# Side products on TensorE in two halves and farther apart: an attention layer whose softmax exponentials run back to back

## What is computed

```python
n = layernorm(x)
q = n @ Wq;  latent = (n @ Wk + n @ Wv) @ W_down_kv
k = latent @ W_up_k;  v = latent @ W_up_v
scores = clip(q_h @ k_h.T * scale) * exp(-1e-4 * |i - j|)      # per head
x = x + softmax(scores) @ v_h (heads joined) @ Wo
m = layernorm(x) in bf16
x = x + (fp8(m / s_in) @ fp8(kernel / s_k) * (s_in * s_k) + bias) in bf16
```

## Time and profile before

| | |
|---|---|
| median of 3 runs | 535.85 us (535.15 to 536.35) |
| the profiled execution, its own time | 536.72 us |
| its span, first to last instruction | 534.9 us |
| ScalarE busy | 490.5 us, 479.9 of it in 512 exponentials |
| TensorE busy (matmuls) | 491.2 us |
| first exponential starts, last one starts | 15.2 us, 513.1 us |
| TensorE's granted clock, mean | 0.985 of full speed |

### The profile page before, as it was taken

How to read it: one execution, slowest core, us unless ns; L and a number is a source line. 1 busy time by engine, 2 the same in 40 slices (tenths; PEclk the granted TensorE clock), 3 DMA queues, 4 the chain that set the end, 5 groups by cost and what they waited for, 6 DMA issues and landing times.

```text
span 534.9 us, 9389 instructions
## 1 busy us (share of the span) xinstructions
PE 491.2 (92%) x3457; PEld 113.1 (21%) x3457; DVE 281.7 (53%) x641; ACT 490.5 (92%) x534; POOL 218.9 (41%) x281
## 2 busy tenths in 40 slices
PE   8778799999999999999999999999999999999961
PEld 3311111231121221231121212222112212122220
DVE  5523754454744555554654555554555545455646
ACT  3769799999999999999999999999999999999961
POOL 0878506974251218993251217994101121002110
PEclk9999999999999999999999999999999999999995
DMA  5388789736997100757987000757987000100000
GB/s 175 128 288 201 237 250 216 259 140 206 257 208 177 50 5 25 276 171 218 256 171 179 8 5 7 263 177 222 260 189 161 26 7 7 45 1 2 1 20 25
DMA packets 49107, 73.79 MB, mean 138 GB/s; under 512 B 6112, under 2 KB 26528, under 8 KB 49056
## 3 DMA queue, kind: packets, MB, share of 16 engines
q1 hardware_dynamic: 48240, 72.85, 49.3%
q10 hardware_dynamic: 816, 0.28, 0.2%
HBM read 35.40 MB, written 35.65 MB: 133 GB/s over the span
## 4 chain that ended last, share of the span: by engine, by line
PE 46%; ACT 29%; issue 8%; DVE 6%; POOL 4%; DMA 3%; SPq 3%; DVEq 0%; POOLq 0%; ACTq 0%
ACT probs L749 28%; PE ps L948 23%; PE ps L932 13%; DVE ps L1173 2%; DMA o_raw<-pv_out 2%; PE ps L850 1%; PE ps L845 1%; PE ps L813 1%; PE ps L788 1%; SPq L442 1%; DMA kp_dram<-parts 1%; PE ps L822 1%; PE ps L817 1%; SPq L445 1%; POOL sq L575 1%
## 5 line engine op out<-in xcount | busy, mean ns | idle before, releaser
L749 ACT ACTIVATE probs<-ps 128x1024 f32<-128x1024 f32 x512 | 479.9, 1064 | 18.3 <-DVE ps L1173 12.5
L948 PE MATMUL ps<-probs,V 128*9 128x512 f32 x2048 | 269.0, 597 | 4.0 <-DVE pv_out L1181 1.5
L1173 DVE TENSOR_TENSOR ps<-ps,consts 128x256 f32<-128x256 f32 (+1 forms) x256 | 144.0, 566 | 179.9 <-PE ps L932 173.1
L932 PE MATMUL ps<-Qs,Ks 64*128 64x512 bf16 x992 | 181.6, 386 | 18.9 <-ACT probs L749 8.3
L932 PEld LDWEIGHTS ps<-Qs,Ks 64*128 64x128 bf16 x992 | 43.8, 93 | 290.6 <-ACT probs L749 269.1
L948 PEld LDWEIGHTS ps<-probs,V 128*9 128x9 f32 x2048 | 31.3, 88 | 79.5 <-issue 58.0
L636 POOL TENSOR_TENSOR xs<-xs,magic 128x512 f32<-128x512 f32 x7 | 8.9, 1276 | 92.5 <-DVE magic L1234 92.5
L553 POOL TENSOR_SCALAR rs<-mv 128x4 f32<-128x4 f32 (+1 forms) x10 | 2.3, 230 | 82.9 <-DVEq L1355 82.3
L575 POOL TENSOR_TENSOR sq<-kT,decay 128x256 f32<-128x256 f32 (+2 forms) x13 | 16.3, 1251 | 47.0 <-DVE kT L1273 31.1
L1181 DVE COPY pv_out<-ps 105x512 f32<-105x512 f32 x31 | 21.4, 691 | 24.7 <-PE ps L948 24.7
L587 POOL TENSOR_TENSOR sq<-sq,parts 128x1024 f32<-128x1024 f32 (+1 forms) x16 | 29.4, 1836 | 1.3
(11 more groups left out here) (148 smaller groups left out, 286.3 us busy)
## 6 DMA issues: line engine op xcount, KB each, us to landing
Qs<-qp_dram SPq DMA_DIRECT2D x26, 512.0 KB, 9.3
qp_dram<-parts SPq DMA_DIRECT2D x16, 768.0 KB, 4.8
Ks<-kp_dram SPq DMA_DIRECT2D x26, 384.0 KB, 6.0
kp_dram<-parts SPq DMA_DIRECT2D x12, 384.0 KB, 3.8
kp_dram<-parts SPq DMA_DIRECT2D x6, 768.0 KB, 4.3
qp_dram<-parts SPq DMA_DIRECT2D x8, 512.0 KB, 6.0
Qs<-qp_dram SPq DMA_DIRECT2D x12, 256.0 KB, 8.4
X<-L_attn_x SPq DMA_DIRECT2D x10, 256.0 KB, 3.0
```

The lines of the kernel that those rows point to most:

```text
L749: nc.scalar.activation(probs[:, quad % RING, 2 * jp:2 * jp + 2, :].rearrange("p j n -> p (j n)"), ps_all[:, bank * CH:(bank + 2) * CH], AC ...
L932: last = nc.tensor.matmul(bank, Ks[half, g, jp, key_cols(v, kc)], Qs[half, g, jp, qh, v, :], start=True, stop=True)
L948: last = nc.tensor.matmul(pv[32 * j:32 * j + VW, :], V[:, unit // 2 * NB + kc, HG * j + g, :], probs[:, quad % RING, j, :], start=i == 0, ...
L1173: nc.vector.tensor_tensor(own, own, factors, ALU.mult).then_inc(fixed, 1)
```

## The change

- Five kinds of side jobs (`sp`, `proj`, `k`, `v`, `n`) and `q` of even number, where they stand at a quad over 8, are made in two parts: the first half of the columns or tiles two quads before the job's quad, the second half at it. There are 33 such jobs (`PARTED`). Both parts go to bank 7; only the second signals VectorE, and only the first waits.
- Jobs are moved so that two full jobs stand four quads apart: in streams 1 and 2 `proj` from 12 to 14, `T` from 14 to 6, `q` from 28 to 30, `xqT` from 30 to 34, `y` from 34 to 36, the second `q` from 36 to 38, `v` from 38 and 46 to 50 and 54. In stream 0 the second `k` goes from 28 to 30, `q` from 30 and 36 to 34 and 38, `v` from 38 and 46 to 50 and 54. In stream 3 `flags` and `flag` go from 14 and 18 to 18 and 20, `turn` from 14 and 18 to 18 and 22.
- VectorE's row statistics go from 13 to 15 and their aggregation from 15 to 17.
- `prepare_weights` runs at quads 21 to 28 instead of 16 to 23. The wait for its result, before at one place of TensorE's loop, is in `multiply`.

```diff
-TAIL_ROWS = [28 if not is_shared(_u) else 34 if _u % 2 else 30 for _u in range(UNITS)]
-TAIL_PRODUCTS = [30 if not is_shared(_u) else 36 if _u % 2 else 34 for _u in range(UNITS)]
+TAIL_ROWS = [34 if is_shared(_u) else 28 for _u in range(UNITS)]
+TAIL_PRODUCTS = [36 if is_shared(_u) else 30 for _u in range(UNITS)]
...
-        (10, "sp"), (12, "proj"), (TAIL_ROWS[_u], "xqT"), (TAIL_PRODUCTS[_u], "y"))]
+        (10, "sp"), (14, "proj"), (TAIL_ROWS[_u], "xqT"), (TAIL_PRODUCTS[_u], "y"))]
...
-        (14, "T", 0), (18, "T", 1), (22 if _b else 26, "k", 0), (26 if _b else 28, "k", 1),
-        (28 if _b else 30, "q", 0), (36, "q", 1), (38, "v", 0), (46, "v", 1))]
+        (6 if _b else 14, "T", 0), (18, "T", 1), (22 if _b else 26, "k", 0), (26 if _b else 30, "k", 1),
+        (30 if _b else 34, "q", 0), (38, "q", 1), (50, "v", 0), (54, "v", 1))]
...
+PARTED = [_j for _j in JOBS if _j[0] > 8 and (_j[1] in ("sp", "proj", "k", "v", "n") or _j[1] == "q" and _j[2] % 2 == 0)]
+PE_SIDE = {_q: (_k, _i, (1,) if (_q, _k, _i) in PARTED else (0, 1)) for _q, _k, _i in JOBS}
+PE_SIDE.update({_q - 2: (_k, _i, (0,)) for _q, _k, _i in PARTED})
...
+            def project_k(n, bank, part=None):
+                if part != 1:
+                    pe.wait_ge(xnT_ready, n + 1)
+                last = nc.tensor.matmul(columns(bank, part), wk_eff[:, :], xnT[:, own_rows(n, part)], start=True, stop=True)
+                if part != 0:
+                    last.then_inc(k_ps, 1)
...
-                elif at == 13:
+                elif at == 15:
                     row_stats(unit)
-                elif at == 15:
+                elif at == 17:
                     row_moments()
...
-                if 16 <= quad < 24:
-                    prepare_weights(quad - 16)
+                if 21 <= quad < 29:
+                    prepare_weights(quad - 21)
```

More of the change, by code:

```diff
@@ L823, in project_v, with head_norms @@
                                             start=True, stop=True)
-                last.then_inc(v_ps, 1)
-            def head_norms(b, bank):
-                pe.wait_ge(sq_ready, b + 1)
-                for a in range(2):
+                if part != 0:
+                    last.then_inc(v_ps, 1)
+            def head_norms(b, bank, part=None):
+                if part != 1:
+                    pe.wait_ge(sq_ready, b + 1)
+                for a in range(2) if part is None else (part,):
                     for half in range(2):
@@ L832, in head_norms @@
                                                 start=True, stop=True)
-                last.then_inc(n_ps, 1)
+                if part != 0:
+                    last.then_inc(n_ps, 1)
             def turn_tops(bank):
@@ L860, in multiply @@
             def multiply(unit, bank):
+                pe.wait_ge(kq_ready, 1)
                 for t in range(4):
@@ L872, in turn_group, with job @@
                 last.then_inc(turn_ps, 1)
-            def job(kind, i):
+            def job(kind, i, part=None):
                 n = JOB_ORDER.index((kind, i))
-                if n > 0:
+                if n > 0 and part != 1:
                     semaphore, value = emptied(*JOB_ORDER[n - 1])
@@ L893, in job @@
                 elif kind == "sp":
-                    spread_sums(i, work)
+                    spread_sums(i, work, part)
                 elif kind == "turn":
@@ L898, in job @@
                 elif kind == "proj":
-                    project_o(i, work)
+                    project_o(i, work, part)
                 elif kind == "xqT":
@@ L982, in _ @@
                         pe.wait_ge(xnT_ready, 2)
-                    if quad == STREAM // 2 + 26:
-                        pe.wait_ge(kq_ready, 1)
-                    job(*PE_SIDE[quad])
+                    kind, i, which = PE_SIDE[quad]
+                    job(kind, i, which[0] if len(which) == 1 else None)
                 if quad == 0:
@@ L989, in _ @@
             weigh(QUADS - 1)
-            pairs = (range(0, 2), range(2, 4))
             for half in range(2):
```

55 lines of the change are left out of this document (32 added, 23 removed).

## The result

| | before | changed |
|---|---|---|
| median | 536.01 us (534.88 to 537.12, 20 runs) | 537.59 us (535.65 to 539.43, 20 runs) |
| ratio, with its 95% interval | | 1.0025 (1.0016 to 1.0034) |
| the profiled execution, its own time | 536.72 us | 538.02 us |
| its span | 534.9 us | 536.2 us |
| TensorE's granted clock, mean | 0.985 | 0.982 |

The change makes the kernel slower by a quarter of a per cent. The forecast was 528.9 us in a range of 524.4 to 533.0; it is 8.7 us off, and of the wrong sign.

The account below looks back on a forecast made before the run. ScalarE was taken as the bound, with small delays by TensorE's backlog. Terms -0.3 - 0.7 + 0.5 - 2.4 - 2.7 - 1.2 - 0.6 + 0.4 = -7.0 us gave 529.7 profiled, 528.9 median; 8-in-10 range 524.4 to 533.0.

Parts of the forecast that it names:

- (c): Halves and distances: -0.7 us in quads 42 to 63, -2.4 and -2.7 in streams 1 and 2, -1.2 in stream 3.
- (a): Weights' steps five quads later, with GpSimd idle: ScalarE's two idle pieces in stream 0 go, -4.05 us.
- (b): Stream 0's late key chain: VectorE stands some 4.5 us at quad 39, the clock falls; net -0.3 us at quad 42.
- (d): Gather landings elsewhere: +0.5 us at quad 71, +0.4 at quads 103, 135, 167 and 199 together.
- -1.4 us: In stream 0, how much earlier the second `k`'s copy, and so the gather landing before quad 39's inversion, would come.
- half a job's length: Term for the second `k`'s copy in stream 0: the cut makes it 0.53 us earlier.
- no stall at quad 39: Rival: the gather comes in time at quad 39, -4.5 us instead of -0.3; 524.7 us, chance 0.05.
- 0.10 us lost a half: ScalarE's loss for each half job, taken from a lone `T`; bounds 0 and 0.24 us.
- cheap halves: Rival: half a job costs 0.59 us or less, so 58 halves lose nothing, -5.8 us; 523.1 us, chance 0.12.
- the gathers take over: Rival: landings stay while quads move, VectorE waits 1 us each in four places; 532.5 us, chance 0.15.
- The added passes become the bound: Rival: 33 cuts add 7.6 us of TensorE time, in full if a half exceeds 0.84 us; 542.6 us, chance 0.03.
- all given back: Rival: distances gain 3.5 us, quad 39's stall is 2 us longer with a second clock fall; 535.5 us, chance 0.06.

Follow-up runs that it names:

- e1: The kernel before with only the weights' steps moved, to quads 21 to 28; 536.61 us, ratio 1.0012.
- e2: The changed kernel with no job cut, all quads kept; 537.36 us, ratio 1.0021.
- e8: The changed kernel with only the 14 jobs cut whose first half stands at a multiple of eight; 537.1 us, one run.
- e3: The changed kernel with those 14 jobs whole whose first half would stand at a multiple of eight, 19 still cut; 535.34 us, ratio 0.9981.
- e4: The changed kernel with stream 0's second `k` whole and back at quad 28; 534.23 us, ratio 0.9962.
- e5: The changed kernel with unit 0's sums inverted at quad 43 instead of 39, `sp` and `proj` whole at 44 and 46; 534.61 us, ratio 0.997.
- e6: The kernel before with weights' steps at 21 to 28, inversions of units 0 and 1 four quads later, one `v` and one `T` moved; 535.5 us, ratio 0.9981.
- e7: The changed kernel without first halves at multiples of eight, inversions of units 0 and 1 four quads later, their `sp` and `proj` whole; 529.63 us, ratio 0.9884.
- e11: The changed kernel with 17 unread matmuls of zeros before TensorE's wait at quad 40; 536.41 us, ratio 1.0011.
- e10: e7 with nine unread matmuls of zeros at quad 8; 528.7 us, ratio 0.9867.
- e12: The changed kernel with unread matmuls of zeros at both quads 8 and 40; 535.47 us, ratio 0.9996.

## Why the prediction was wrong, point by point

On the profiled executions the sum said -7.0 us and +1.3 came. Of the 8.3 between, (c)'s terms hold 7.4 (streams 1 and 2 5.1, quads 42 to 63 1.5, stream 3 0.8), the net of (a) and (b) at quad 42 holds 2.2, (d) was 1.5 too high, and 0.2 lies behind the last exponential.

**(a) The weights' steps: right.** -4.05 us forecast, -4.16 in quads 16 to 32, and -4.3 in e1, where nothing else moved. Each step costs VectorE 0.2 to 0.3 us there; one fix, at 74.82, starts straight behind a step.

**(b) The key chain: the mechanism was right, the net wrong by 2.2 us.** "20.6 us from copy to landing" was 20.65, "stands some 4.5 us" was 4.39, "I expect its clock to fall again; ... 1.1" was 0.96. The step that failed is "-1.4 us" for the copy's start. The copy came at 84.41, 1.2 us later than before instead of 1.4 earlier, and exponential 80 at 106.87 instead of near 104.3: outside the bound of 106 that was named as the sign of an error. Counted from the start of quad 8, and less the 1.47 us of the clock's fall in front, the copies tell the terms apart: 44.22 us before, 39.89 in e1 (the weights' steps, -4.33), 43.45 in e2 (two quads later and the distances, +3.56), 44.12 in the changed kernel (the halves, +0.67). So the two quads' +3.62 and the weights' -4.05 were right; the spacing's 0.45 was worth 0.06; and "half a job's length", -0.53, was +0.67, because the second half does end sooner but the first halves push its quad back by more. With the first `k` alone cut (e8) the copy is at 43.74, with the second alone (e3) at 43.80. VectorE's copy in e2, then in e3:

```profile
82.22 0.69 DVE L1301 COPY kT<-ps 128x512 f32<-128x512 f32 x1 [0.62 <-PE ps L829]
```
```profile
81.46 0.69 DVE L1302 COPY kT<-ps 128x512 f32<-128x512 f32 x1 [0.19 <-PE ps L830]
```

The copy follows the start of its product by 1.16 us in e2 (81.06) and by 0.73 in e3 (80.73), 0.43 sooner; but that start, counted from quad 8's (38.77 and 37.66), is 0.78 later. The rest of the miss is the fall of the clock at 39 us, 1.47, seen in some executions and not in others, and 0.2 of an earlier start. Without that fall exponential 80 is at 104.67 and 103.86 in e2 and e3, near the forecast's 104.3, but e3 owes that to a start of quad 8 that is 1.3 us earlier than before: luck. The net at quad 42 (exponential 84 at 111.20 against 109.29) became +1.9, not -0.3.

**What (b) never asked** is whether the chain moves with the program at all. The text took the landing as copy plus a length. e1 and e4 show a length that grows as the copy comes earlier: 22.8 us for a copy at 77.79, 21.9 at 79.43, 20.6 at 83.22. The prediction's rival "no stall at quad 39", 524.7 us, did not come true in the two runs that had the keys earlier, and the blame laid on the keys' two quads was only partly deserved: with the keys back (e4) 2.26 us of wait remained, and 2.30 opened at quad 71.

**(c) Halves and distances: here most of the 8.7 us lie.** The term for half a job, "0.70 of TensorE's time", measured 0.74: nearly right. The term "0.10 us lost a half" was wrong where it mattered. It was made from a lone `T` in open country, and it ignored at which quads the halves would stand. Before, no side job stood at a multiple of eight; the change put 14 first halves there, and on average over the four of stream 2 each costs 0.24 us more than a whole job at 8k+2 does, through a wait of TensorE for VectorE's copy of bank 6 (behind eight of the 14). The others gain 0.45 over six. Together a stream gained 0.2 to 0.4 us instead of 2.4 to 2.7, and in stream 1 even the 0.4 is not theirs: the 0.6 that quad 71 lost before is gone there. The distances were over-valued too: "the distance does the work", but alone (e2) they took 0.7 us off stream 2. In quads 40 to 64 the excess without the clock's share was 2.5 against 2.0 before, where 1.3 was forecast. Two halves cost 1.48 us here against 1.17 for the whole, so the rows decide for the dearer half, and the rival "cheap halves" falls. The Trainium skill (TensorE: Matmul & The Clock Gate, the section on why a matmul takes 56 and not 53.3 ns) has back-to-back matmuls start N columns' time plus about 2.5 ns apart; by that rule alone two halves would cost little more than one whole, and the trace does not agree.

In stream 3 the forecast was -1.8 us with `flags`; -1.02 came.

**(d) Gathers elsewhere: wrong in sign, and small.** The loss at quad 71 was to grow by 0.5 us and vanished: the program had not gained, so the landing was in time. That is luck of the other errors. e5 shows that the reasoning itself was good, with 4.49 us of wait as soon as the program did gain. No gather was waited for at quads 103 or 135, so "the gathers take over" did not come about. It did in e4 and e5, in another guise.

**The rivals on the slow side.** "The added passes become the bound" needed a half above 0.84 us; it was 0.74, streams 1 and 2 got shorter, not longer, and TensorE's busy time grew by 4.0 us, not 7.6. The nearest was "all given back", 535.5 us at a chance of 0.06: the distances gain a part, and a second fall of the clock comes. But it wanted a stall 2 us longer at quad 39 with the second fall there, and that did not come: the second fall was in front. The chance for anything but faster was set at 0.08, and only this rival let (b) and (c) fail together, as they did.

**What stays open.** Why the clock falls at 39 us in some executions and not in others was not settled; e6, e7 and the changed kernel show it in their profiles, the kernel before and eight others without fillers don't. The length of the idle piece doesn't tell them apart: TensorE waits 2.0 to 2.2 us there in the three, and as long in the kernel before, e2, e4 and e11. That fillers there remove it fits the profiles and the narrower spread of e10 and e12, but rests on few executions; that the changed kernel meets it more often than the kernel before is not shown. What the second wall at quad 71 consists of was not tested either.

## What to carry to other kernels

A gain in one stage is worth only what the next fixed point lets through: before adding up gains, list what comes from outside the program's own pace (a landing, a queue behind bulk loads), and ask at which time it would come if everything before it were faster. When a long job is cut, look where the pieces fall among the hand-overs of other engines: a piece just ahead of an accumulation bank's last product cost more here than the whole job did two quads later, and whole jobs put there (e6) did harm as well. And where a stall can't be removed, matmuls that nobody reads can keep TensorE's clock through it; here they lengthened nothing.

## What the runs showed of the hardware

- In the profiles a fall to half clock (1.2 GHz) came behind every stall of TensorE at quad 40 in which VectorE waited 2.67 us or more and no fillers ran (the changed kernel, e1, e2, e3, e8), not in e4, with 2.26 us. It lasted 3.4 us and cost 0.96 us at quad 40, 1.3 to 1.5 us at quad 8. The mean clock varies between executions of one kernel, and the time with it: in e1 two groups of runs, their nearest members 1.0 us apart and their farthest 3.4.
- The landing of one 16 KB gather took 1.97 us with the DMA engines 0.23 busy, 5.31 us with 0.96, and 4.96 us in e4, where the engines were busy at first and idle for the last 1.7 us.
- A float32 job of 512 columns between score products cost 1.17 us, one of 256 columns 0.74: by a straight line through the two, an estimate, 0.31 us does not depend on the columns.
- Behind side products placed right ahead of the last sum into bank 6, TensorE waited 0.36 to 0.37 us for VectorE's copy of the bank: behind eight of the 14 halves in the changed kernel, and behind both whole jobs in e6.
- The scaling of 128 columns on VectorE took 1.98 us beside GpSimd's product and 0.28 with GpSimd idle.
